# First two units of a recurrence in the plain eight-part form instead of the seven-product form, in a kernel of 32 units on one core

## The reference

```
ft = sigmoid(xt @ wf.T + c @ uf.T + bf);  it = sigmoid(xt @ wi.T + c @ ui.T + bi)
gt = tanh(xt @ wc.T + c @ uc.T + bc);     c = ft * c + it * gt
```

## Time and profile before

| | us |
|---|---|
| median of 3 runs | 2634.09 (2632.4 to 2635.8) |
| profiled execution | 2635.06 |
| its span | 2633.4 |
| PE busy | 2524.9 (96%) |
| PE weight load busy | 2203.9 (84%) |
| DVE busy | 1834.9 (70%) |
| ACT busy | 1627.5 (62%) |
| POOL busy | 1127.6 (43%) |

### The profile page before, as it was taken

One profiled execution on the slowest core, in us unless ns is written; L12 is line 12 of the kernel. 1 busy time (PEld: TensorE's weight loads), 2 busy tenths in 40 slices (PEclk: granted clock), 3 DMA queues, 4 the chain that ended last, 5 costly groups with the idle time before them and its releaser, 6 DMA issues.

```text
span 2633.4 us, 57587 instructions
## 1 busy us (share of the span) xinstructions
PE 2524.9 (96%) x22659; PEld 2203.9 (84%) x22659; DVE 1834.9 (70%) x3411; ACT 1627.5 (62%) x3013; POOL 1127.6 (43%) x1437
## 2 busy tenths in 40 slices
PE   5599999997999999999999999999999999999998
PEld 4378888886788888888888888888888888888887
DVE  7865656558886777767777887776677764467667
ACT  8766767666665555555557665555555553379777
POOL 7878677724332223222234432322223220068667
PEclk9799999998999999999999999999999999999999
DMA  8879778889664565445655755544556432489998
GB/s 353 322 236 335 263 264 296 296 299 331 162 179 117 138 147 157 117 114 138 151 157 157 208 146 144 162 119 115 136 134 171 117 85 49 161 339 351 368 358 346
DMA packets 507551, 542.52 MB, mean 206 GB/s; under 512 B 273936, under 2 KB 412944, under 8 KB 488720
## 3 DMA queue, kind: packets, MB, share of 16 engines
q1 hardware_dynamic: 507280, 538.85, 65.7%
HBM read 292.88 MB, written 180.88 MB: 180 GB/s over the span
## 4 chain that ended last, share of the span: by engine, by line
PE 84%; DVE 4%; ACT 3%; DMA 2%; issue 1%; POOL 1%; SPq 1%; DVEq 0%; ACTq 0%; POOLq 0%
PE bank L2178 31%; PE bank L2188 29%; PE bank L2234 8%; PE bank L2067 4%; PE bank L2017 3%; PE bank L2053 3%; PE bank L2075 3%; PE bank L2029 2%; PE bank L2209 2%; DVE big L1859 1%; PE bank L2037 1%; ACT big L1360 1%; DVE big L1916 1%; DMA x1d<-big 1%; DVE big L1902 0%
## 5 line engine op out<-in xcount | busy, mean ns | idle before, releaser
L2178 PE MATMUL bank<-big 128*128 128x256 f16 x8064 | 1081.3, 274 | 18.3 <-ACT big L1406 7.9
L2188 PE MATMUL bank<-big 128*128 128x256 f16 x7056 | 962.5, 273 | 0.0
L2178 PEld LDWEIGHTS bank<-big 128*128 128x128 f16 x8064 | 791.7, 98 | 116.1 <-ACT big L1406 9.6
L2188 PEld LDWEIGHTS bank<-big 128*128 128x128 f16 x7056 | 690.4, 98 | 79.9
L1042 POOL TENSOR_SCALAR big<-big 128x1 f32<-128x1 f32 x253 | 108.1, 427 | 1088.0 <-DVE big L1706 810.9
L1916 DVE TENSOR_TENSOR big<-bank,big 128x512 f32<-128x512 f32 x256 | 174.9, 683 | 197.6 <-PE bank L2188 193.5
L2234 PE MATMUL bank<-big 128*128 128x256 f16 x2688 | 295.3, 273 | 4.4 <-ACT bank L1340 4.0
L1316 ACT ACTIVATE big<-big 128x512 f32<-128x512 f32 x384 | 289.6, 803 | 12.6 <-DVE big L1916 12.6
L2234 PEld LDWEIGHTS bank<-big 128*128 128x128 f16 x2688 | 262.4, 98 | 36.9 <-ACT bank L1340 4.9
L1902 DVE TENSOR_TENSOR big<-bank,big 128x512 f32<-128x512 f32 x256 | 176.1, 688 | 143.1 <-PE bank L2188 119.4
L1248 ACT ACTIVATE big<-big 128x512 f32<-128x512 f32 x256 | 206.4, 808 | 105.1 <-POOL big L1044 101.6
(11 more groups left out here) (236 smaller groups left out, 3715.2 us busy)
## 6 DMA issues: line engine op xcount, KB each, us to landing
xtd<-big SPq DMA_DIRECT2D x60, 1024.0 KB, 6.7
big<-xr SPq DMA_DIRECT2D x16, 2048.0 KB, 9.2
big<-xg SPq DMA_DIRECT2D x64, 512.0 KB, 7.7
big<-kpad SPq DMA_DIRECT2D x32, 1024.0 KB, 12.3
yd<-big SPq DMA_DIRECT2D x16, 2048.0 KB, 16.8
big<-x SPq DMA_DIRECT2D x128, 256.0 KB, 3.2
x1d<-big SPq DMA_DIRECT2D x128, 256.0 KB, 3.2
big<-x1d SPq DMA_DIRECT2D x64, 512.0 KB, 8.5
```

Source lines behind the costliest of these rows:

```text
L2178: ins = e.matmul(o, WX[2 * g + lw][:, q, kt, 128 * a:128 * a + 128], slot[u % 2][:, part, lx, k0 + kt, :], start=(first and kt == 0 and (l ...
L2188: ins = e.matmul(o, WC[2 * g + lw][:, q, kt, 128 * a:128 * a + 128], cc[unit(u)[1] % 2][:, qc, lx, kt, :], start=False, stop=end, skip_gro ...
```

## The change

- Units 0 and 1 (`PLAIN_UNITS = 2`) and the four head pairs of these two units (`PLAIN_PAIRS`) are computed in the plain form: 8 block products, 48 matmuls per group, 24 for each of two banks (`plain`, `head_plain`). No partial sums are copied or added for them: ACT applies the gates, or the head's tanh, straight from the banks (`gates_plain`, `head_tanh`), and a bank is free once that is done (`bank_free`). Everything that counted groups now counts those that are not plain (`before`, `closed`, `finished`).
- The plain form needs three blocks that are among the 7 parts, and block W12 itself, an eighth part (`f = 7`). It is made for `n % 4 == 2` from W12 before POOL replaces it, stored to `w12d` and loaded to `WX12`. POOL's fourth sum becomes `last_sum`, which stands between the normalizations of its group. The places of the parts change for `n % 4 == 2`.
- Unit 0's rows have 4 items instead of 8: 16 transposes on PE instead of 32, no `first_sums`. Unit 1 has 4 items and 4 transposing transfers instead of 8, staged in four buffers (`staged`), and no sums. `store_xt` stores half as much for both.
- The transfers at the start of the recurrence stand in another order: the weights `WX[4]`, `WX[5]` and the third eighth part ahead of unit 1's `x` rows, unit 2's `x` rows ahead of `WC[3]` and `WC[4]`, and `x` rows of units 1 and 2 wait for single chunks.
- ACT and DVE do the steps for units 1 and 2 earlier (`SPECIAL`), unit 2's by a group of units.

```diff
@@ weight_places @@
-                behind = (7, 8, 9, 11, 12, 13, 14) if n == 2 else (4, 5, 6, 8, 9, 11, 13)
-                places = [("hi", q, n, behind[q]) for q in range(7)] + [("lo", q, n, min(behind[q] + 1, 15)) for q in range(7)]
+                behind = (7, 9, 10, 11, 12, 13, 14, 8) if n == 2 else (4, 6, 7, 8, 9, 11, 13, 5) if n % 4 == 2 else (4, 5, 6, 8, 9, 11, 13)
+                places = [("hi", q, n, a) for q, a in enumerate(behind)] + [("lo", q, n, min(a + 1, 15)) for q, a in enumerate(behind)]
@@ SPECIAL @@
-    1: {"dve": ((0, 0), (0, 0), (0, 0), (0, 0), (0, 2), (0, 3), (2, 1), (2, 3), (2, 3), (3, 2), (3, 3), (4, 3), (4, 3), (5, 3), (5, 3), (5, 3), (5, 3), (5, 3)),
-        "act": ((1, 0), (1, 1), (1, 2), (2, 0), (2, 1), (2, 1), (2, 2), (2, 2), (3, 1), (3, 2), (4, 0), (5, 1), (6, 0), (6, 0), (6, 0), (6, 0))},
-    2: {"dve": ((5, 3), (5, 3), (5, 3), (6, 0), (6, 0), (6, 2), (7, 0), (7, 2), (7, 2), (8, 0), (8, 2), (9, 0), (9, 0), (9, 2), (9, 2), (9, 2), (10, 2), (10, 2)),
-        "act": ((6, 0), (6, 0), (6, 0), (6, 2), (7, 0), (7, 1), (7, 1), (7, 2), (8, 0), (8, 2), (8, 2), (9, 0), (9, 1), (9, 2), (10, 2), (10, 2))},
+    1: {"dve": ((0, 0), (0, 0), (0, 0), (0, 0), (0, 1), (0, 1), (0, 2), (0, 3), (0, 3), (9, 0), (1, 0), (9, 0), (9, 0), (9, 0), (1, 1), (1, 1), (9, 0), (9, 0)),
+        "act": ((0, 0), (0, 0), (0, 0), (0, 0), (0, 1), (0, 1), (0, 2), (0, 2), (1, 0), (9, 0), (9, 0), (1, 1), (1, 2), (1, 2), (9, 0), (9, 0))},
+    2: {"dve": ((4, 2), (4, 3), (5, 0), (5, 0), (5, 2), (5, 3), (6, 0), (6, 2), (6, 2), (7, 0), (7, 0), (8, 0), (8, 0), (8, 2), (8, 2), (8, 2), (9, 2), (9, 2)),
+        "act": ((5, 0), (5, 0), (5, 1), (5, 2), (6, 0), (6, 0), (6, 1), (6, 1), (7, 0), (7, 2), (7, 2), (8, 0), (8, 1), (8, 2), (9, 2), (9, 2))},
-POOL_SUMS = (1, 2, 16, 17, 18, 19)
+POOL_SUMS = (2, 16, 17, 18, 19)
@@ pool_program @@
-                for o, p0, p1 in ((Wt[0], W12, W11), (Wt[1], W22, Wt[0]), (W12, W22, W12), (Wt[2], W21, Wt[1])):
+                for o, p0, p1 in ((Wt[0], W12, W11), (Wt[1], W22, Wt[0]), (Wt[2], W21, Wt[1])):
                     ws().tensor_tensor(o, p0, p1, SUB).then_inc(s["w_sum"], 1)
+
+            def last_sum(n):
+
+                m = 2 * (n // 4) + n % 2
+                if m % 2 == 0:
+                    w.wait_ge(s["w_hi"], high_base(m) + 2 * cut_place(m, 7) + 2)
+                    w.wait_ge(s["w_lo"], low_base(m) + cut_place(m, 7) + 1)
+                ws().tensor_tensor(W12, W22, W12, SUB).then_inc(s["w_sum"], 1)
 
             for i in range(1, NG - 1):
                 for q in range(4):
                     if i % 4 >= 2 and q == 0:
                         quarter_sums(i)
+                    if i % 4 == 3 and q == 0 or i % 4 == 2 and q == (3 if i == 2 else 2):
+                        last_sum(i)
                     norm(4 * (i + 1) + q)
@@ act_program, weights @@
+        SUMMED = {3: 1, 4: 2, 5: 4, 6: 3}
...
-                                if f >= 3:
-                                    w.wait_ge(s["w_sum"], 4 * m + f - 2)
+                                if f in SUMMED:
+                                    w.wait_ge(s["w_sum"], 4 * m + SUMMED[f])
+                                if f == 6 and m % 2 == 0:
+                                    w.wait_ge(s["w12"], 16 * (m // 2 + 1))
@@ act_program, gates of a plain group @@
+            def gates_plain(n):
+                u, gi = divmod(n, 6)
+                a, g = divmod(gi, 3)
+                w.wait_ge(s["yc"], 3)
+                room(n)
+                bs = bias0 if unit(u)[0] == 0 else bias
+                for r in range(2):
+                    w.wait_ge(s[("pa", "pb")[r]], n + 1)
+                    e.activation(zt[g][:, r::2, :], (bank_a(n), bank_b(n))[r][:, :].rearrange("p (q t) -> p q t", q=2), ACT.Tanh if g == 2 else ACT.Sigmoid,
                                  bias=bs[:, g, a + 2 * r:a + 2 * r + 1], scale=inv[g]).then_inc(s["ga"], 1)
@@ pe_program, a plain group @@
+            def plain(n, r, o, sem):
+
+                u, gi = divmod(n, 6)
+                a, g = divmod(gi, 3)
+                w.wait_ge(s["wx"], 16 * (6 if g == 2 else 4))
+                if r:
+                    w.wait_ge(s["w12"], 16 * (6 if g == 2 else 5))
+                for h in range(2):
+                    w.wait_ge(s[f"xq{h}"], 32 * u)
+                    for k in range(2):
+                        for kt in range(2):
+                            for lw, lx in PARTS:
+                                end = k == 1 and kt == 1 and (lw, lx) == PARTS[-1]
+                                part = WX[2 * g + lw][:, WHOLE[k, r]] if (k, r) in WHOLE else WX12[g][:, lw]
+                                ins = e.matmul(o[:, 256 * h:256 * h + 256], part[:, kt, 128 * a:128 * a + 128], slot[u % 2][:, h, lx, 2 * k + kt, :],
+                                               start=(h == 0 and k == 0 and kt == 0 and (lw, lx) == PARTS[0]), stop=end, skip_group_check=True)
+                                if end and h:
+                                    ins.then_inc(s[sem], 1)
@@ sync_program, transfers at the start of the recurrence @@
+            w.wait_ge(s["w12"], 16 * 4)
+            e.dma_start(f16(x1_at + 4096, 1024).rearrange("p (g x) -> p g x", g=2), w12d[0:2].rearrange("g p l x -> p g (l x)")).then_inc(s["w12"], 16)
             for r in range(4):
                 store_x1(0, r)
             load_y(1)
-            for c in CHUNKS:
-                load_x1(1, c)
             w.wait_ge(s["wx"], 16 * 4)
             load_WX(4)
             load_WX(5)
+            w.wait_ge(s["w12"], 16 * 5)
+            e.dma_start(f16(x1_at + 5120, 512), w12d[2].rearrange("p l x -> p (l x)")).then_inc(s["w12"], 16)
+            for c in CHUNKS:
+                load_x1(1, c)
@@ act_program, k == 10 @@
-                    w.wait_ge(s["kscl"], 1)
+                    w.wait_ge(s["gs"], 1)
```

More of the change, by code:

```diff
@@ L219, with before, closed, plain_at @@
 LOADED = [U for U in range(NU) if U % 8 or U >= 16]
+PLAIN_UNITS = 2
+PLAIN_PAIRS = tuple(m for m in range(PAIRS) if head_unit(m // 2) < PLAIN_UNITS)
+PLAIN = tuple(range(6 * PLAIN_UNITS)) + tuple(GROUPS + m for m in PLAIN_PAIRS)
+WHOLE = {(0, 0): 0, (1, 0): 1, (1, 1): 2}
+def before(n):
+    return n - sum(m < n for m in PLAIN)
+def closed(k):
+    return k + 1 - sum(place(m) <= k for m in PLAIN)
+def plain_at(k):
+    return next((m for m in PLAIN if place(m) == k), None)
+def finished(n):
+    return ("pb", n + 1) if n in PLAIN else ("p7", before(n + 1))
+def first_item(v):
+    return 8 * v - 4 * min(v, PLAIN_UNITS)
+def sums_before(v):
+    return 8 * (v - PLAIN_UNITS)
+def turns_before(v, k):
+    return 2 * (v - 1 if k < 2 else v - PLAIN_UNITS)
 def state_parts(u):
@@ L268, in prep_schedule @@
                 g += 6 * v - 9
-            at[g, place].append((step, v))
+            if v >= PLAIN_UNITS or step not in ((9, 11, 12, 13, 16, 17) if engine == "dve" else (9, 10, 14, 15)):
+                at[g, place].append((step, v))
     return at
@@ L1282, in prepare @@
                     norm2(n + (4, 5, 8, 11).index(step))
+                elif v < PLAIN_UNITS:
+                    high(i + (6, 7, 12, 13).index(step))
                 else:
@@ L1326, in act_program, with bank_free @@
             norm2(3)
-            for i in range(2, 8):
+            for i in range(2, 4):
                 high(i)
             w.wait_ge(s["yc"], 2)
+            def bank_free(n):
+                k = place(n) - 4
+                w.wait_ge(s["u1"], closed(k))
+                w.wait_ge(s["u2"], closed(k))
+                m = plain_at(k)
+                if m is not None:
+                    w.wait_ge(s["th"], m - GROUPS + 1)
             def head_seed(m):
@@ L1740, in prepare @@
                         rows_sums(w, ss, v, (9, 13).index(step))
+                elif v < PLAIN_UNITS:
+                    low(i + (7, 8, 14, 15).index(step))
                 else:
@@ L1906, in dve_program @@
                     head_stat(m - 2, 1)
-                if 0 <= m < PAIRS:
+                if 0 <= m < PAIRS and n not in PLAIN:
                     head_fifth(m)
@@ L2236, in head_product, with head_plain, whole @@
                             ins.then_inc(s[sem], 1)
+            def head_plain(m, r, o, sem):
+                U, p = divmod(m, 2)
+                i = LOADED.index(U)
+                b = i % NXR
+                w.wait_ge(s["wq"], 32)
+                w.wait_ge(s["w12"], 16 * 7)
+                w.wait_ge(s[f"xr{b}"], 48 * (i // NXR + 1))
+                xw = (xu0[b], xu23[b][:, 0])[r]
+                for f in range(2):
+                    for k in range(2):
+                        for kt in range(2):
+                            for lw, lx in PARTS:
+                                end = k == 1 and kt == 1 and (lw, lx) == PARTS[-1]
+                                part = Wq[lw][:, WHOLE[k, f]] if (k, f) in WHOLE else Wq12[:, lw]
```

(9 more changed lines are left out.)

344 lines of the change are left out of this document (193 added, 151 removed).

## The result

The changed kernel takes 2639.93 us (median of 13 runs, 2637.06 to 2640.54) against 2633.65 us (13 runs, 2631.73 to 2635.8): ratio 1.0021, 95% interval 1.0014 to 1.0028. It is slower by 0.2%, where 0.3% faster was forecast, and lies outside the range (2619.5 to 2636). The profiled executions are 5.0 us apart (spans 2638.4 and 2633.4 us).

What follows compares the result with a forecast made beforehand. PE's matmul count was taken as the bound, except at the recurrence's start, where PE waits and the transfers' share is 1.00. Terms 6.2 + 0.3 - 16.0 + 2.6 = -6.9 us gave 2627.2 us, range 2619.5 to 2636.

Steps and rivals of the forecast that it cites:

- Third sequence group: ACT waits 5.2 us for POOL's moved weight sum, PE is late and loses 1.0 at half clock: 6.2 us lost.
- Groups 6, 10, 14: Weight sum hidden with 2 us over; the eighth part costs 0.1 us each, 0.3 in all.
- Start of the first unit: Without sums and with half the transposes it starts at 600.15 us; 1.65 lost to the clock, no weight wait.
- The plain groups: First two units: 12 groups of 48 matmuls at 0.1085 us take 62.5 us instead of 54.7.
- Third unit: Begins at 665.8 us instead of 681.8, with 1.5 us of waiting in all before it: gain 16.0 us.
- The walk through the rows' steps: Step times for second and third units' rows (third: norms at 651, then POOL's sums), margins 0 to 3 us.
- Rival (2): Second unit's rows land 3 to 5 us late, delaying the third: gain 8 to 10; 0.24 together with Rival (4).
- Rival (4): Plain units save no waits, ACT being four groups late; same time as Rival (2), 0.24 together.
- Rival (3): Transfers bound the recurrence's start, so the third unit begins at 681.8 us as before: 2643.2 us; chance 0.09.
- The sign set for a failure: Wrong if ACT does not idle near 188 us, or third unit comes over 88 us after the last sequence matmul.
- rival 1: No wait for the weight sum in the third sequence group: 2621.0 us; chance 0.15.
- Head: Four plain head pairs add 24 matmuls on a busy PE: 2.6 us more.

Runs made afterwards that it cites:

- runs 1: Changed kernel with the third sequence group's last weight sum ahead of the second normalization instead of the fourth: 2632.33 us, ratio 0.9992.
- run 9: The run 6 kernel with ACT's and DVE's steps for the third unit back at the groups of the kernel before: 2631.94 us, ratio 0.999.
- run 7: Changed kernel with the last weight sum of groups 6, 10 and 14 ahead of the fourth normalization too: 2643.67 us, ratio 1.0036.
- run 6: Changed kernel with the edits of runs 1 and Run 4, plus two third-unit transposes issued ahead of the fourth unit's loads: 2624.02 us, ratio 0.9964.
- Run 4: Changed kernel with the second unit's 1 MB store and three 0.9 MB weight loads put behind the third unit's row stores: 2633.53 us, ratio 0.9996.
- run 3: Changed kernel with only the 1 MB store of the second unit's transposed rows issued behind the third unit's rows: 2637.29 us, ratio 1.0007.
- run 10: Changed kernel without one of eight block products in each of the four plain head pairs (24 matmuls): 2637.55 us, ratio 1.0009.
- run 2: Changed kernel with the third sequence group's last weight sum ahead of the third normalization instead of the fourth: 2633.58 us, ratio 0.9994.

## Why the prediction was wrong

The forecast was 6.9 us less; the two spans say 5.0 more. Of the 11.9 us between them 7.2 stand at the third unit, 2.1 at the third group, 1.3 in groups 6, 10 and 14, and 1.5 behind the mark, less the 0.2 us named under the table.

**Third sequence group: mechanism right, size off.** Of the 6.2 us forecast 8.3 came. The 5.2 us of wait were counted from weights that landed at 172.7 us; in this execution they landed at 175.0 (in the traces of eight of the ten experiments at 174.9 to 175.4, in those of runs 1 and 9 at 172.8 and 173.4), and the wait was 6.92. In after the load was issued at 166.8 us instead of 165.2, because the issue of the store ahead of it (`accd`) took SP 2.9 us instead of 1.1; why the loads mostly land late stays open. After the pause the matmuls were at half clock from 196.2 to 200.8 us, so some 2.3 us were lost to it, against the 1.0 taken from a shorter pause. (By the earlier trace rows that one had its clock at half from 613.5 to 616.9 us, not from 613.3 to 616.6, 1.7 us lost.) The Trainium skill (TensorE: Matmul & The Clock Gate, Part 1) has an idle TensorE fall back to 1.2 GHz and earn 2.4 GHz again; the trace agrees, with 6.37 us of pause, 0.95 of which PE had before, and 8.3 us of loss. It is not so for every pause: one of 1.65 us (run 9) cost only itself.

**Groups 6, 10, 14: a term mis-sized.** 0.64, 0.46 and 0.46 us instead of 0.1 each. The sum itself is hidden with 3 us over (run 7); so what costs is the eighth part's own work, most likely ACT's 1.3 us in each group. That was not isolated.

**Start of the first unit: right.** It begins 15.84 us after the last sequence matmul (forecast 16.3), and no weight is waited for. The plain groups took 65.2 us where 62.5 and 1.65 for the clock had been counted, 1.05 more: the clock was at half until 613.9 us, some 2.2 us lost, and a matmul took 0.1091 us (537 in 58.60 us) and not 0.1085. In run 6 the first 4.73 us, 23 matmuls, are at 0.51.

**Third unit: the step that failed.** The prediction put 1.5 us of waiting in all ahead of the second and the third unit, and 665.8 us as the third's beginning. The second unit waited for nothing; at the third there were 5.5 us of wait and 2.6 us of half clock behind it (36 matmuls in 6.57 us instead of 3.93): 8.1. With 1.05 us more at the start and 0.4 less before it, this makes the 7.2 us by which the gain fell short. The walk through the rows' steps had the loads' bytes in it for the second unit, but for the third it had "norms at 651, POOL's sums after them" without asking when the rows that the sums overwrite are stored; the sums began at 658.2 us in after, 8.0 us after POOL was free for them. Run 4 shows that the answer was in the queue, in five transfers of about 1 MB ahead of the stores; run 3 moves one of them for part of the gain.

Rival (2) had this place and this mechanism (sums waiting for stored rows, a gain of 8 to 10 us), but it began with a delay of the second unit's rows. These did land 3.3 us later than the 610.8 us counted (the last at 623.3, less the 9.2 us by which the first unit began later than forecast), and that unit still waited for nothing. The Trainium skill (DMA: Bandwidth & Descriptors, Two DMAs through the same engine are not ordered) says that within one queue of one DMA engine transfers start in order; ten landings in the order of issue, and landing times of 12.4 us that fall to 4.5 once 3.7 MB stand behind the stores, agree with that. It speaks for waiting behind what was issued earlier, which is what happened, and not for the rival's sharing with loads issued behind the rows. Rival (4) falls: no plain group waited for its gates. Rival (3), the transfers as the bound, falls in its strong form: in run 6 nearly the same bytes are moved, and the third unit waits for none. The sign set for a failure did not show: the third unit came 86.6 us after the last sequence matmul, more than the 82 forecast but not above 88, and its half clock lies behind that point.

What the change was to save up to the third unit does come once both losses are mended: in run 6 that unit begins 65.1 us after the first, where the prediction has 65.65. Two errors cancel in this, no wait instead of 1.5 us, and 1.05 us more for the clock and the price of a matmul. Run 6 is 15.9 us under the changed kernel. Forecast and run 6 differ by 3.2 us the other way, since there the third group's loss is gone too. By the prediction's terms without that loss it would be 2621.0 (its rival 1), 13.1 us less than before; run 6's span (2622.2 us) is 11.2 less. The 1.9 us between: 1.2 more in the sequence stage, 0.4 from the third unit's beginning to the mark and 1.2 from there to the head (the term that follows below), less 0.9 up to the third unit. The medians differ by 1 us more, which their intervals allow.

**Head: right.** 2.6 us forecast and seen, and given back in run 10's trace.

**From the mark to the head: 1.5 us that no term had.** In 1380 to 1500 us, where the schedule for units 16 to 19 changes, PE is busy 116.87 us in the changed kernel and 118.32 before.

The stretch with most of it, before and after:

```profile
1400.00:1420.00 20.00, 19.49 (x179) 17.23 (x177) 16.54 (x26) 15.01 (x27) 1.35 (x3) 1.00 0.94 188
1400.00:1420.00 20.00, 18.60 (x171) 16.43 (x170) 14.75 (x24) 14.75 (x27) 1.33 (x3) 1.00 1.01 179
```

ACT waits there 1.63 us for a transposing transfer where it waited 0.39, with the same four transposes issued in 6.38 instead of 5.38 us. All ten experiments have it (PE busy 116.7 to 117.4 us there), so it comes with the change; what in it does this stays open.

## What to carry to other kernels

When steps are moved earlier, follow the chain back to its first link that the move does not touch, a transfer in a queue above all: count the bytes issued ahead of it, and move those that are needed last behind it. A step placed earlier than its input can come can be worse than one placed late, since it holds up everything behind it in its engine's list: the same move cost 3 us in one kernel and gained 8 in another. And a sum or a copy taken out of a list has a due time: count when its reader comes, in normalizations, before choosing its place.

## What was not expected of the hardware

- The time to landing of a 256 KB store: 4.5 us with one 1 MB store and 0.5 MB of rows issued just ahead, 12.4 us with 4.7 MB and the same rows.
- After PE's pauses of 6.4 and 5.5 us the first matmuls were at half rate, for 4.7 and 5.4 us. After one of 3.0 us (run 4) they began at full rate, fell to half 1.0 us later and were back after 3.4 us more, and so after one of 1.95 us in the kernel before (0.9 and 3.4 us). After one of 1.65 us (run 9) they did not fall before the next pause, but after two of 1.62 and 1.29 us close together (run 2) they did. The length of one pause alone does not tell.
- The same load of weights landed at 172.7 to 173.4 us in three traces and at 174.9 to 175.4 in the nine others.
